# A gated cross-attention kernel: operands of the middle stage prepared inside the first attention, and VectorE's work there moved to other steps

## What is computed

```python
x = x + tanh(g_xattn[0]) * L0_xattn(ctx, layernorm(x), mask, ...)   # 16 heads of 64; keys: context rows, then the tokens
x = x + tanh(g_ffn[0])   * L0_ffn(layernorm(x), ...)                # 8 experts of 128, the best two of each token
x = x + tanh(g_xattn[1]) * L1_xattn(layernorm(x), ctx, ...)         # 16 heads of 16; keys: context rows
x = x + tanh(g_ffn[1])   * L1_ffn(layernorm(x), ...)                # quantised gate, up and down, 1024 wide
```

## Time and profile before

| | |
|---|---|
| median of three runs | 3250.26 us (3250.1 to 3251.94) |
| the profiled execution | 3252.86 us, its span 3251.1 us |
| busy share of the span | TensorE 91%, VectorE 74%, GpSimd 65%, ScalarE 56% |
| granted clock of TensorE | 0.973 of full speed |
| first attention, unit 0 to the end of unit 31 | about 93 to 2313 us |
| middle stage up to its first expert step | 2313.7 to 2394.6 us |

### The profile page before, as it was taken

One profiled execution on the slowest core, in us unless ns is written; L12 is line 12 of the kernel. 1 busy time (PEld: TensorE's weight loads), 2 busy tenths in 40 slices (PEclk: granted clock), 3 DMA queues, 4 the chain that ended last, 5 costly groups with the idle time before them and its releaser, 6 DMA issues. The chain is left out here.

```text
span 3251.1 us, 53579 instructions
## 1 busy us (share of the span) xinstructions
PE 2952.4 (91%) x21712; PEld 1091.0 (34%) x21720; DVE 2419.8 (74%) x2991; ACT 1806.9 (56%) x2025; POOL 2118.1 (65%) x1017
## 2 busy tenths in 40 slices
PE   5899999999999999999999999999498699999988
PEld 3233333333333333333333333322355123333235
DVE  8776787677777767777777876774435888888878
ACT  4455555455445555545555554545344388888875
POOL 5787988897898888889888888999520111111114
PEclk8999999999999999999999999999699699999999
DMA  1000000000000000000000000000210100000000
GB/s 62 6 1 1 1 8 1 1 7 1 1 7 1 1 1 7 1 1 7 1 1 1 3 1 1 1 1 1 68 33 9 46 7 7 8 7 7 7 1 27
DMA packets 24616, 28.73 MB, mean 9 GB/s; under 512 B 6511, under 2 KB 21296, under 8 KB 24370
## 3 DMA queue, kind: packets, MB, share of 16 engines
q1 hardware_dynamic: 24370, 25.31, 2.6%
HBM read 17.42 MB, written 2.10 MB: 6 GB/s over the span
## 5 line engine op out<-in xcount | busy, mean ns | idle before, releaser
L348 POOL TENSOR_TENSOR a_acc<-a_acc,a_prob 128x1024 f32<-128x1024 f32 x704 | 1725.3, 2451 | 299.5 <-ACT a_prob L480 217.7
L598 DVE TENSOR_REDUCE a_part_max<-wide 128x2 f32<-128x1024 f32 x880 | 1069.1, 1215 | 446.1 <-PE wide L885 445.3
L480 ACT ACTIVATE a_prob<-slot,a_mask_bias 128x1024 f32<-128x1024 f32 x928 | 986.9, 1112 | 740.7 <-PE slot L914 721.4
L929 PE MATMUL bank<-a_prob,a_val 128*64 128x512 f32 x3712 | 898.0, 606 | 2.1 <-ACT a_prob L480 2.1
L1218 ACT ACTIVATE a_prob<-slot,a_mask_bias 128x1024 f32<-128x1024 f32 x416 | 455.2, 1115 | 67.4 <-PE slot L1418 54.3
L885 PE MATMUL wide<-a_k_hi,a_q_hi 64*128 64x512 f16 (+1 forms) x2016 | 353.0, 362 | 113.8 <-DVE a_part_max L598 105.9
L1262 DVE TENSOR_REDUCE a_part_max<-wide 128x1 f32<-128x512 f32 x514 | 333.2, 682 | 37.7 <-PE wide L1406 21.0
L929 PEld LDWEIGHTS bank<-a_prob,a_val 128*64 128x64 f32 x3712 | 226.6, 136 | 394.2 <-issue 289.2
L914 PE MATMUL slot<-a_q_hi,a_k_lo 64*128 64x512 f16 x1856 | 352.7, 377 | 0.0
L914 PE MATMUL slot<-a_q_hi,a_k_step_hi 64*128 64x512 f16 x1728 | 328.2, 377 | 2.6 <-ACT a_prob L480 2.5
L914 PE MATMUL slot<-a_q_lo,a_k_step_hi 64*128 64x512 f16 x1728 | 328.0, 376 | 0.0
(11 more groups left out here) (398 smaller groups left out, 3275.0 us busy)
## 6 DMA issues: line engine op xcount, KB each, us to landing
a_w_staged<-in_w SPq DMA_DIRECT2D x8, 384.0 KB, 3.2
x_res<-in_x SPq DMA_DIRECT2D x4, 512.0 KB, 5.8
a_q_op<-a_hi SPq DMA_DIRECT2D x128, 16.0 KB, 1.8
out_x<-x_res SPq DMA_DIRECT2D x16, 128.0 KB, 1.7
a_k_op<-mid_k_hi SPq DMA_DIRECT2D x32, 52.0 KB, 2.2
mid_context<-in_ctxt SPq DMA_DIRECT2D x1, 1601.0 KB, 6.6
mid_w_staged<-in_w1a SPq DMA_DIRECT2D x4, 384.5 KB, 6.4
a_acc<-in_ctx SPq DMA_DIRECT2D x3, 512.0 KB, 8.4
```

The lines of the kernel that those rows point to most:

```text
L348: nc.gpsimd.tensor_tensor(acc, before, prob[:, k % R, :], ALU.add).then_inc(added_p, 1)
L480: nc.scalar.activation(prob[:, k % R, :], m.slot[k % 2][:, :], ACT.Exp, bias=mbias[:, t:t + 1]).then_inc(probs_ready, 1)
L598: nc.vector.reduce_max(part_max[:, w % 2, :, j, c], pairs, AX.X).then_inc(max_used, 1)
L929: ins = nc.tensor.matmul(av[r, :], val[g % 2][:, t, r], prob[:, k % R, h * QB:(h + 1) * QB], start=(t == 0), stop=(t == NT - 1), tile_posi ...
```

## The change

Five things, in one diff:

1. **Order of VectorE's work in a unit.** The reciprocals go to steps 11, 13, 15, 17, the division to step 17, the output products to steps 19 and 21 (residuals 20 and 22), the key steps of a job to four steps behind it (three at steps 0 to 2). VectorE's tiles are 3, 5, 7, 19, 21, so its additions run at steps 7, 9, 21, 23.
2. **Last unit.** VectorE's tiles are nine (`end_tiles`). GpSimd no longer joins the halves: the sums take both. Reciprocals and division run in two halves, each followed by its own output product in a bank of its own.
3. **Middle stage's operands.** Context, the weights of groups 0 and 1, router, small expert parts and biases are fetched when unit 28's values are done; GpSimd sets constants in unit 29, ScalarE makes `hi` parts in unit 30, VectorE the `lo` parts and the bias operand in unit 31, and the statistics of three quarters of `x` at step 23 of units 29 to 31. They lie in memory that the first attention no longer uses by then (buffers of even groups).
4. **Middle stage.** Key jobs of groups 0 and 1 stand first, without waiting for operands; two `ones_of` stand first on GpSimd; one root and one reciprocal serve all 16 tiles; groups 2 and 3 of weights are asked for at once.
5. **Opening.** Two projections, not five, stand ahead of the first raw products; the context's transposes come at pairs 2, 6, 10, 14 instead of 0, 4, 8, 12; GpSimd's fill waits for all normalisations.

```diff
-        self.sums_at, self.invert_at, self.pieces, self.divide_at, self.out_at = 9, 12, 4, 16, (17, 19)
+        self.sums_at, self.invert_at, self.divide_at, self.out_at = 9, (11, 13, 15, 17), 17, (19, 21)
-        self.dve_tiles = [5, 7, 9, 15, 17]
+        self.dve_tiles = [3, 5, 7, 19, 21]
+        self.end_tiles = [3, 5, 7, 9, 13, 17, 21, 25, 27]
+        self.front_at = [(3, "scale", 0), (5, "keys", 0), (7, "queries", 0), (9, "scale", 1), (11, "keys", 1), (13, "queries", 1),
+                         (15, "router", 0)] + [(17 + 2 * c, "context", c) for c in range(4)]
+        self.low_at = [(1, "keys", 0), (2, "queries", 0), (3, "keys", 1), (4, "queries", 1), (5, "context", 0), (6, "context", 1),
+                       (7, "context", 2), (8, "context", 3), (13, "context", 4), (14, "context", 5), (15, "context", 6), (17, "context", 7),
+                       (19, "router", 0), (22, "bias", 0)]
...
+            sp.wait_ge(av_done, (last - NU + 1) * NT)
+            sp.dma_start(front.c32[:, :, 0:CTX], front.context.rearrange("(c p) t -> p c t", p=P)).then_inc(front_c, 16)
+            for g in range(2):
+                sp.dma_start(front.w_st[:, g, :], front.w_in[g, :, :]).then_inc(front_w, 16)
+            for to, source in front.small:
+                sp.dma_start(to, source).then_inc(front_small, 16)
...
-            for n in range(6):
-                row_low(n)
+            row_low(2)
+            row_low(3)
+            pool.wait_ge(normed, len(cols))
...
-            add_up(a.units - 1)
+                    if w == last - 2 and t == 3:
+                        pool.wait_ge(front_c, 16)
+                        nc.gpsimd.memset(front.c32[:, :, CTX:CTXP], 0.0).then_inc(front_set, 1)
...
+                    if w == last - 1:
+                        for at, what, n in a.front_at:
+                            if t == at:
+                                prepare(what, n)
...
-                    if w and 0 <= t - a.invert_at < a.pieces:
-                        invert(w - 1, t - a.invert_at)
+                    if w and t in a.invert_at:
+                        invert(w - 1, a.invert_at.index(t))
...
-                    if k - 3 in a.job_at and a.job_at[k - 3][1] < a.nkq:
-                        step_low(*a.job_at[k - 3])
+                    ago = 3 if t < 3 else 4
+                    if k - ago in a.job_at and a.job_at[k - ago][1] < a.nkq:
+                        step_low(*a.job_at[k - ago])
+                    if w > last - NU + 1 and t == a.out_at[1] + 2:
+                        measure_final(w - (last - NU + 2))
+                    if w == last:
+                        for at, what, n in a.low_at:
+                            if t == at:
+                                prepare_low(what, n)
...
-            for piece in range(a.pieces):
-                invert(a.units - 1, piece)
-            divide(a.units - 1)
+            for z in range(2):
+                for piece in range(a.pieces // 2):
+                    invert(last, a.pieces // 2 * z + piece)
+                divide_half(last, z)
...
+                if w == last:
+                    pe.wait_ge(added_v, sum_v(w))
+                    pe.wait_ge(added_p, sum_p(w))
+                    parts = [acc_v, acc_p]
...
-            turn_rows(2)
-            project(0, a.open_jobs[2])
-            turn_rows(3)
-            project(0, a.open_jobs[3])
-            project(0, a.open_jobs[4])
...
-        kinds = [("k", 0)] + [("v", g) for g in range(self.groups)] + [("k", g) for g in range(1, self.groups)]
+        kinds = [("k", 0), ("k", 1)] + [("v", g) for g in range(self.groups)] + [("k", 2), ("k", 3)]
...
-            turn(0, 0)
-            turn(0, 1)
-            project(0)
-            turn(0, 2)
-            project(1)
-            turn(0, 3)
-            project(2)
-            project(3)
+            for b in range(NB):
+                project(2 * b)
+                project(2 * b + 1)
+                turn(0, b)
```

More of the change, by code:

```diff
@@ L344, in add @@
                 if n == 0:
-                    before = prob[:, (w * NT + a.pool_tiles[0]) % R, :]
+                    before = prob[:, (w * NT + tiles[0]) % R, :]
                 else:
@@ L626, in add @@
                 if n == 0:
-                    before = prob[:, (w * NT + a.dve_tiles[0]) % R, :]
+                    before = prob[:, (w * NT + tiles[0]) % R, :]
                 else:
@@ L942, in outputs @@
                 g = w // NU
-                free_side(("out", w, z))
+                if w < last:
+                    free_side(("out", w, z))
+                else:
+                    pe.wait_ge(att_ready, w + z + 1)
+                    pe.wait_ge(probs_ready, S)
                 if z == 0:
@@ L980, in _ @@
                     n = w * NT + t + a.lead
+                    if w == 0 and t == 0:
+                        scores(w, t)
+                        pair(n)
+                        continue
                     if t % 2 == 0:
@@ L1003, in _ @@
                         project(*a.job_at[w * NT + t])
-            last = a.units - 1
             values(last, NT - 2)
@@ L1046, in stage_cross @@
         wo = sb("wo", [P, a.groups, D])
-        bo, bos = sb("bo", [P, D]), sb("bo_gated", [P, D])
-        y = sb("y", [P, a.stage, 512])
+        y = keep.late[:, 0:a.stage * 512].rearrange("p (s q) -> p s q", s=a.stage)
+        bo, bos = keep.late[:, a.stage * 512:a.stage * 512 + D], sb("bo_gated", [P, D])
         hi, lo = sb("hi", [P, a.stage, 512], FP16), sb("lo", [P, a.stage, 512], FP16)
@@ L1788, in _ @@
                 weights_high(g)
-                evacuate(NC + a.routing + g)
-            for p in range(NC + a.routing + NB, a.nj):
+                evacuate(a.front + a.routing + g)
+            for p in range(a.front + a.routing + NB, a.nj):
                 evacuate(p)
```

480 lines of the change are left out of this document (272 added, 208 removed).

## The result

| | before | after |
|---|---|---|
| median | 3250.26 us | 3232.34 us (3231.24 to 3234.79, five runs) |
| ratio | | 0.9946, 95% interval 0.9931 to 0.9960 |
| span of the profiled execution | 3251.1 us | 3229.7 us (the execution itself 3231.74) |

The change makes the kernel 18 us faster, 0.55%. The forecast was 52 us, with 3168 to 3231 as its range: the sign is right, the size is not, and the time lies 1 us outside.

What follows compares the result with a forecast made beforehand. TensorE was taken to lead in the first attention, with GpSimd close behind. Opening -7, first attention -18, last group +4, last unit and tail -10, middle stage -21 gave -52 and a likeliest 3198 us, range 3168 to 3231.

Steps and rivals of the forecast that it cites:

- First attention: Units 0 to 27: moved additions stall TensorE less, saving 2.6 us per group of four, times seven: -18.
- step 17: Each first-attention unit: reciprocal and division there overrun the free time, a new TensorE stall of 0.42 us.
- 2.09 for an addition: First attention: price in us taken for each VectorE addition at its new step, from a median row of 2.17.
- the key steps (0.77): First attention: price in us per key step, moving from even to odd steps.
- +25 from the longest row: First attention's upper bound: if each addition takes 3.02 us, units pay 0.9 more, times 28.
- the slower rival: GpSimd becomes the bound with eleven additions in a row, 27 us slower, 3277; decides from 2.8 an addition; chance 0.05.
- the one with +5: Rival that the rhythm brings nothing: +5 in place of -18, the last unit gives 5, 3226 us; chance 0.20.
- units over 68.8 us: Sign in the units that the prediction is wrong: they last longer than 68.8 us, their length before the change.
- Opening: Before unit 0: VectorE's idle 7.30 us before its first context row goes, -7; ends 2 and 11.
- Last group: Units 28 to 30: uncovered statistics add 3.5 us, GpSimd waits 0 to 3 for context; sum +4, ends 0 and +9.
- Last unit and tail: GpSimd's additions end 6 to 7 us earlier, splits giving back 6.5; tail 8.2 to 11; -10, ends -3 and -19.
- Middle stage: Routing some 23 us after its start, GpSimd's early ones end ScalarE's waits, expert steps at 60; -21, ends -10 and -26.

Runs made afterwards that it cites:

- b_adds: The kernel before with VectorE's additions alone moved to tiles 3, 5, 7, 19, 21; 3251.67 us, ratio 1.0000.
- a_key3: The changed kernel with every key step done three steps after its projection again instead of four; 3217.11 us.
- a_div16: The changed kernel with reciprocals at steps 11, 12, 13, 15 and the division at step 16, so step 17 has neither; 3214.65 us.
- a_mix_ones16: a_mix with GpSimd's settings of ones and weights' zeros held back until all sixteen middle-stage normalisations are done; 3186.01 us, ratio 0.9795.
- a_none: The changed kernel with additions, reciprocals, division, outputs and key steps put back to their old places; 3218.68 us, ratio 0.9896.
- a_mix: The changed kernel with old reciprocals, division, outputs and key steps; old addition places only in third units and units 28, 29; 3190.40 us, ratio 0.9813.
- b_key4: The kernel before with key steps alone moved from three to four steps behind their projection; 3310.52 us, ratio 1.0182.

## Why the prediction came out as it did

**First attention: wrong, and in effect the whole error.** It is 35.7 us off; the other parts are off by -6.8, -3.2, +3.0, +4.7 and -2.8 and nearly cancel. The counting of steps was sound where no two-input operation of VectorE met GpSimd. It gave 0.42 for step 17 (0.64), and nothing for steps 13 and 15 (nothing). In the second and fourth units it gave 1.3 less (0.8 and 0.7, since 0.45 stayed behind step 9). What failed is the price list. I took "2.09 for an addition" and "the key steps (0.77)" as fixed. They are 1.2 and 0.3 to 0.7 plus what is left of GpSimd's running addition, and in the worst meeting a whole one: at steps 7 and 9 of the third unit the additions took 3.06 and 3.01, and a key step up to 2.66. A median holds only at the places where it was measured, and the change moved just these operations. Nor was 2.17 the median of "128 like rows": the earlier trace rows has 96 of them, the other 32, the first addition of each unit, had 2.41 and went up to 3.17, and all 128 together 2.25. In the first unit I forecast 1.6 less and got 0.2 more, in the third 1.1 more and got 4.0 more.

A slip came on top: the third unit's last key step lands on step 11, beside a reciprocal. I had written "they land on steps 7 and 9", and the 1.23 us behind step 11 is this.

With the rows' own prices the same count comes out. In the third unit shown above it gives 3.06 + 0.68 - 0.16 - 1.40 = 2.2 behind step 7, 3.01 + 0.68 - 0.16 - 2.01 = 1.5 behind step 9 and 0.95 + 1.48 - 0.16 - 1.05 = 1.2 behind step 11, where 2.13, 1.65 and 1.23 stand.

By parts, a group: my count gives the additions' move alone some 8 us less (0.1 a unit, in place of 8.7 in four units). b_adds measured 0.6 less: 3.8 less in three units and 3.2 more in the third. To key steps and step 17 it gives some 5 more (0.6, 2.4 and four times 0.42), and they cost 3.3 together. So it is the additions' move that brought far less than its term. Taking back either of the other two edits gives nearly all of their 3.3 (15.2 us by a_key3, 17.7 by a_div16), so these cannot be divided between them.

**The bound held, the range did not.** I had bounded this term at +25 from the longest row, and +17.7 is inside, though the longest addition was then 3.38, not the 3.02 of that bound. But the case that carried the upper end was the one with +5, so the range stopped at 3231. The sentence that would have warned stood in the prediction itself: units over 68.8 us make it wrong. They are 69.4 on average (2152.7 over 31). GpSimd as the bound, the slower rival, did not come: its mean addition is 2.47 us and its decision point was 2.8.

**Opening: right in kind, twice the size.** The idle row of 7.30 us is gone, since the reductions of the first two steps no longer stand behind context rows. The first reduction starts at 32.06 where it started at 47.43, and 1.6 us of that are lost again before unit 0's shift. My upper end was 11. No run took this part by itself, so how the 13.8 divide among the reordered steps stays open.

```profile
start us, us, engine line op out<-in xcount [idle before <-releaser]
31.45 0.69 DVE L636 SCALAR_TENSOR_TENSOR front_arena<-slot,front_arena 128x512 f16<-128x512 f32 x1 [0.56 <-ACT front_arena L498]
32.06 1.21 DVE L669 TENSOR_REDUCE a_part_max<-wide 128x2 f32<-128x1024 f32 x1
```

**Last group**: +0.8 against +4, within its ends. One of its terms rested on a misreading, in the prediction and in the list of changes: SP waits for the values of unit 27, not 28 (`av_done` of 28 x 29). The transfers began at 2043.67, at unit 28's start, the context landed 6.7 us later, and GpSimd, which needs it in unit 29, did not wait. **Last unit and tail**: -7.0 against -10. The sums start 65.8 us after the unit's last shift row instead of 72.0, which are the 6 to 7 forecast, by two errors that cancel: the splits give back 2.7 instead of 6.5, so other terms gave less than I had put. The tail is 11.2 long instead of 12.1. I had 8.2 to 11, but the eight sums take 3.68 us and the last output 2.07, both at a granted clock of 0.50, where the output between them takes 1.13 at 1.00.

**Middle stage**: -16.3 against -21. The logits came after 25.7 us, not 23, and the expert steps after 64.5, not 60. The missing part is the one that I had called gone: GpSimd's early settings of ones. They no longer hold ScalarE, whose wait for the laying out of keys is not in the trace any more, but they hold VectorE's normalisations, 5.3 us by a_mix_ones16. That is more than the 2.7 missing at the logits, so the rest of my 23 was too high. I had named ScalarE as late next, and it was VectorE.

## What to carry to other kernels

An operation of VectorE that reads two tiles in SBUF beside a GpSimd busy with additions has no fixed price: take its undisturbed time and add what is left of the GpSimd instruction running at its start. Where two such operations follow each other and GpSimd has a backlog, that is nearly a whole one for the second. Edits of the order around such operations can then not be priced one by one: a_key3 and a_div16 each gave back nearly all that both together had cost. A pattern that repeats by group should be tuned by unit: one set of places for all units gave nothing (b_adds, 1.0000), the better of two sets for each unit gave 28 us (a_none to a_mix). A helper's constants and memory settings should wait until the engine on the path is through, and all the way through.

## What the runs showed of the hardware that was not expected

- A second two-input operation of VectorE in a row pays for nearly a whole GpSimd addition when GpSimd has several to do: 2.43 us for a subtraction of 128 columns that takes 0.28 alone, and 4.07 us of TensorE's idle time at the worst place in b_key4. In the changed kernel a subtraction of 512 columns behind an addition, at 1077.35, took its undisturbed 0.68, as GpSimd had nothing to run.
- Whichever of the two starts second waits for the rest of the other's operation, but the sums are not equal. In the changed kernel VectorE's additions and key steps lost 192 us in all and GpSimd's additions 84, each counted over its undisturbed time. In the last unit the thirteen splits took 1.2 to 2.85 us, and taking twelve of them out gave GpSimd's chain only 2.7 us in all.
- A GpSimd instruction that only writes SBUF holds VectorE up too, here a normalisation with one tile as input: 0.33 us alone (2.67 for eight) and 1.46 beside the settings (5.83 for four), while four settings took 6.05 us there against 5.76 in a_mix_ones16, where no normalisation ran beside them. The Trainium skill (SBUF — State Buffer, section Who interferes with whom) says that VectorE in its two-port modes and GpSimd block each other for whole instructions. The rows agree with that; which mode these normalisations run in, no row shows.
